# Graph kernel, adjacency build: attribute steps taken in pairs in every second strip, four buffers for the destination one-hots

## The reference, cut to what matters

```python
# x (3125, 128); src, dst (103125,), sorted by dst; edge_attr (103125, 16)
h = jnp.maximum(_layernorm(x), 0.0)
for l in range(5):
    edge_emb = edge_attr @ ew.T + eb
    agg_x = segment_sum(h[src], dst, n) + h
    agg_e = segment_sum(edge_emb, dst, n) + eb
    z = concatenate([agg_x, agg_e], axis=1) @ w1.T + b1
    z = relu((z - mean(z)) * rsqrt(var(z) + 1e-5) * bn_w + bn_b)
    h = z @ w2.T + b2          # relu after layers 0 to 3
return x + h
```

## Time and profile before

| what | value |
|---|---|
| median of 3 runs | 722.11 us |
| the three runs | 726.42, 719.08, 722.11 us |
| the profiled execution, its own time | 723.33 us |
| span of its trace | 721.5 us |
| mean granted clock of TensorE | 0.969 |

### The profile page before, as it was taken

How to read it: one execution, slowest core, us unless ns; L and a number is a source line. 1 busy time by engine, 2 the same in 40 slices (tenths; PEclk the granted TensorE clock), 3 DMA queues, 4 the chain that set the end, 5 groups by cost and what they waited for, 6 DMA issues and landing times.

```text
span 721.5 us, 13619 instructions
## 1 busy us (share of the span) xinstructions
PE 649.8 (90%) x5338; PEld 411.5 (57%) x5338; DVE 382.1 (53%) x807; ACT 260.7 (36%) x627; POOL 89.6 (12%) x62
## 2 busy tenths in 40 slices
PE   0688899898999996989999799997999997999976
PEld 0567678675666663475555665553855556555546
DVE  3699999998999996752120440212421204311124
ACT  0135457675666661470110620113510106201132
POOL 3431226692101110000000000000000000000000
PEclk9899999998999999899999999999999998999998
DMA  8680000000000000000000000000000000100032
GB/s 211 176 261 2 3 2 3 2 3 0 3 1 1 2 1 3 0 8 24 2 1 0 1 29 0 0 0 0 29 0 0 0 0 0 29 2 1 1 89 90
DMA packets 16617, 17.67 MB, mean 24 GB/s; under 512 B 6777, under 2 KB 10786, under 8 KB 16562
## 3 DMA queue, kind: packets, MB, share of 16 engines
q1 hardware_dynamic: 12284, 13.64, 6.4%
q0 software_dynamic: 3440, 1.66, 1.0%
q10 hardware_dynamic: 838, 1.60, 0.8%
HBM read 15.26 MB, written 1.60 MB: 23 GB/s over the span
## 4 chain that ended last, share of the span: by engine, by line
PE 55%; DVE 3%; ACT 1%; issue 0%; POOLq 0%; DVEq 0%
PE bank L961 37%; PE bank L1025 9%; PE bank L996 7%; PE bank L990 2%; DVE bn_stats L1189 1%; ACT h L1079 1%; DVE h L1210 0%; PE bank L1001 0%; ACT aggT L1070 0%; DVE h L1211 0%; ACT bn_small L1092 0%; PE bank L1008 0%; DVE h L1229 0%; DVE bound_row L1169 0%; DVE bn_small L1205 0%
## 5 line engine op out<-in xcount | busy, mean ns | idle before, releaser
L961 PE MATMUL bank<-adj,h_pieces 128*128 (+1 forms) x1400 | 270.8, 353 | 0.0
L961 PEld LDWEIGHTS bank<-adj,h_pieces 128*128 128x128 f16 x1400 | 135.8, 97 | 134.2 <-issue 8.7
L1189 DVE BATCH_NORM_STATS2 bn_stats<-bank 128x6 f32<-128x450 f32 (+1 forms) x70 | 43.8, 629 | 233.9 <-PE bank L996 230.0
L640 ACT ACTIVATE adj<-bank 128x450 bf16<-128x450 f32 x175 | 96.3, 550 | 99.6 <-PE bank L532 99.0
L1070 ACT ACTIVATE aggT<-bank 128x450 f32<-128x450 f32 x28 | 15.3, 546 | 275.9 <-PE bank L996 242.4
L532 PE MATMUL bank<-h 128*128 128x150 bf16 x1050 | 102.3, 234 | 12.8 <-DVE h L301 11.2
L301 DVE TENSOR_TENSOR h<-iota_a,key_a 128x900 bf16<-128x900 bf16 x175 | 110.3, 630 | 0.0
L532 PEld LDWEIGHTS bank<-h 128*128 128x128 bf16 x1050 | 73.0, 99 | 54.2 <-DVE h L301 41.2
L301 DVE TENSOR_TENSOR h<-iota_lo,h 128x768 bf16<-128x768 bf16 x175 | 99.6, 569 | 3.8 <-PE bank L532 1.9
L555 PE MATMUL bank<-h,adj 128*17 128x40 f32 (+11 forms) x1752 | 77.9, 201 | 21.6 <-DMA adj<-attr 19.3
L555 PEld LDWEIGHTS bank<-h,adj 128*17 128x17 f32 x1752 | 68.4, 100 | 31.4 <-DVE h L412 22.1
(11 more groups left out here) (115 smaller groups left out, 307.8 us busy)
## 6 DMA issues: line engine op xcount, KB each, us to landing
adj<-attr SPq DMA_DIRECT2D x5, 1402.5 KB, 15.9
weights<-wpack SPq DMA_DIRECT2D x5, 323.0 KB, 3.2
out<-h SPq DMA_DIRECT2D x6, 256.0 KB
h<-mpack SPq DMA_DIRECT2D x5, 179.0 KB, 2.4
adj<-dst SPq DMA_DIRECT2D x1, 412.5 KB, 12.5
adj<-first SPq DMA_DIRECT2D x1, 201.0 KB, 3.7
adj<-dst_lin,row_index POOLq DMA_INDIRECT x5, 6.8
adj<-pair,start_index POOLq DMA_INDIRECT x5, 11.2
```

Of the source, the lines that this page charges most:

```text
L640: nc.scalar.activation(out_view(u), bank_view(u % CNT_BANKS), ACT.Copy, accum_out=tot[:, u:u + 1]).then_inc(s_ev, 1)
L961: last = nc.tensor.matmul(agg_ps[b][:, 0:CW], hp[:, k, s, :], adj[:, k, ds(c * CW, CW)], start=(k == 0 and s == 0), stop=stop and s == PIE ...
L1189: V.bn_stats(stats[:, h, ds(c * 6, 6)], w1_ps[b][h][:, 0:cols]).then_inc(st_last if last and h == 1 else st_done, 1)
```

## The change

A new constant `DST_SLOTS = 4` gives `dst_oh` four buffers; step `i` on DVE now waits for step `i - 4`. A new function `steps_at(u)` says which steps stand in strip `u`: none in even strips, `u + 3` and `u + 4` in odd ones. DVE and PE both go by it. `step_strip` follows: a chunk that was finished in an even strip now counts from the next odd one. The scratch begins at chunk 1 of `agg0` instead of chunk 3, since four buffers need more room. The number of instructions of each kind is the same.

```diff
+DST_SLOTS = 4
...
+def steps_at(u):
+
+    return [i for i in (u + LEAD - 1, u + LEAD) if i < STEPS] if u % 2 else []
+
+
 def step_strip(i):
 
-    return max(i - LEAD, 0)
+    return max(i - LEAD + (i - LEAD + 1) % 2, 0)
...
-            tail = 3 * CW
+            tail = CW
             sums = agg0[0:REC, tail:tail + CW]
-            dst_oh = agg0[:, tail + CW:tail + CW + SLOTS * RUN * DW].rearrange("p (b x) -> p b x", b=SLOTS)
-            at = tail + CW + SLOTS * RUN * DW
+            dst_oh = agg0[:, tail + CW:tail + CW + DST_SLOTS * RUN * DW].rearrange("p (b x) -> p b x", b=DST_SLOTS)
+            at = tail + CW + DST_SLOTS * RUN * DW
...
-                        if i >= SLOTS:
-                            dve.wait_ge(s_step, i - 1)
+                        if i >= DST_SLOTS:
+                            dve.wait_ge(s_step, i - DST_SLOTS + 1)
...
-                        if u + LEAD < STEPS:
-                            dst_one_hots(u + LEAD)
+                        for i in steps_at(u):
+                            dst_one_hots(i)
...
-                        if u + LEAD < STEPS:
-                            attr_step(u + LEAD)
+                        for i in steps_at(u):
+                            attr_step(i)
```

More of the change, by code:

```diff
@@ L407, in dst_one_hots @@
                     def dst_one_hots(i):
-                        if i >= SLOTS:
-                            dve.wait_ge(s_step, i - 1)
+                        if i >= DST_SLOTS:
+                            dve.wait_ge(s_step, i - DST_SLOTS + 1)
                         k, t = i // 3, (i % 3) * RUN
-                        V.tensor_tensor(dst_oh[:, i % SLOTS, :].rearrange("p (q w) -> p q w", q=RUN),
+                        V.tensor_tensor(dst_oh[:, i % DST_SLOTS, :].rearrange("p (q w) -> p q w", q=RUN),
                                         iota_d.unsqueeze(1).to_broadcast([P, RUN, DW]),
@@ L556, in attr_step @@
                                                         attr_i[:, k, t * REC:(t + 1) * REC],
-                                                        dst_oh[:, i % SLOTS, q * DW + a - c0:q * DW + b - c0],
+                                                        dst_oh[:, i % DST_SLOTS, q * DW + a - c0:q * DW + b - c0],
                                                         start=opens, stop=True, skip_group_check=True)
```

## The result

| | before | changed |
|---|---|---|
| first comparison, median | 722.56 us (4 runs) | 729.62 us (4 runs) |
| first comparison, ratio and 95% interval | | 1.0093 [1.0059, 1.0128] |
| second comparison, median | 723.93 us (23 runs) | 728.32 us (7 runs) |
| second comparison, ratio and 95% interval | | 1.0080 [1.0043, 1.0117] |
| profiled execution, its own time | 723.33 us | 728.73 us |

The ratio is an estimate of its own and not the quotient of the two medians (728.32 / 723.93 is 1.006). By it the change makes the kernel 0.8 to 0.9% slower; the medians lie 7.1 and 4.4 us apart. I had forecast no change, with 728.0 us as the upper end of the range.

What follows compares the result with a forecast made beforehand. DVE, which never rests, was taken to set the build's pace. Terms 0 + 0.1 + 0.5 + 0 = +0.6 us on the profiled 723.33 gave 723.9, in terms of the median 722.7 us, no change; range 717.5 to 728.0 us.

Steps and rivals of the forecast that it cites:

- Part 1: Attribute steps in pairs in the build: DVE needs 3.06 us for two strips before and after; no net gain, 0.
- Part 2: The stack's matmuls on PE, now always behind two attribute steps: DVE may wait, +0.1 us, bounds 0 and 0.5.
- Part 3: Step moved past keys and starts at the end of strip 10: DVE loses +0.5 us, bounds 0 and +0.5.
- Part 4: POOL beside DVE in the build: they lock each other out, equally often in both kernels, so 0.
- rival 1: POOL starves until strip 74, first products on PE start late: +4.4 to +6.3, 727.1 to 729.0 us; chance 0.10.
- Rival 2: PE's clock falls to 1.2 GHz, priced over strips 10 to 17: +6.4 us, 729.1 us or more; chance 0.08.
- rival 3: POOL finishes low pieces while DVE waits anyway, PE's clock does not fall at 160 to 166: 718.2 us; chance 0.10.

## Why the prediction was wrong

**Part 1 held.** Two one-hots stand together, two strips take 3.07 us (from 127.71 to 130.78 us), DVE's wait ahead of the strips is gone and the one for the first pairs grew from 3.19 to 5.58 us, where I forecast about 5.2. Four buffers alone changed nothing.

**Part 2 held.** From the first one-hot to strip 73 the trace lists no wait of DVE for PE. What I missed is that the waits of 0.06 us, which I counted as no cost, had a use.

**Part 3 held in size and missed a place.** The keys' wait grew from 1.44 to 1.79 us and strip 12 began 0.4 us late, where I took 0.5; but since it stays with pairs in even strips, the cause that I gave is not confirmed. Another fixed wait stood at strip 38, where DVE now waits 0.53 us for ACT's deviation, which ACT begins at 106.18 instead of 105.17, behind a copy of the stack that the pairs had moved next to it: 0.6 us that were not in the sum. With pairs in even strips it is gone.

**The step that failed is Part 4's "so I take 0"**, and behind it the sentence in rival 1 that "the gap that let POOL in comes from strips 70 on, which the change leaves as they are". The trace before has two gaps, near 129.8 and 160.7. I priced the second and did not ask what had opened the first, which stood between the row of 114.56 and that of 130. It was the slack of 1.54 us used up by the stack; the pairs put two one-hots between, the gap closed, and POOL was shut out for 43.7 us. Pairs without the extra buffers do it, and holding POOL back in the old order costs the same, 728.5 us. The term that I took as 0 measured 1.4 us in the build of the first profile (6.1 won up to strip 74, 7.5 lost behind it) and 2.4 us in the second (6.1 and 8.5); the other 1.0 and 1.3 us of the build had been lost by strip 40.

**Rival 1 was the right mechanism, at a chance of 0.10.** It had the wait at strip 74 and 727.1 to 729.0 us. PE waited 6.40 us at the first product, which came at 170.02 instead of the 171.4 that I had worked out. PE did restart at its lower clock, as the rival's upper end supposed, until 172.9. The build lost 2.4 and 3.6 us in two profiles, less than the 4.4 of the rival: DVE came to strip 74 at 159.82, 5.1 us ahead of the kernel before and not 2.0, and POOL got in there, 3 us before PE began to count that strip at 162.69.

**The rest of the profiles' difference is the layers' clock, which was no term at all.** In the first profile it brought 3.0 of 5.4 us, in the second 0.7, and since it moves from execution to execution, neither is shown to be an effect of the change. I had read the granted clock as a matter of the build alone. What stays open is how the medians divide: they differ by 7.1 and 4.4 us, the builds of the profiles by 2.4 and 3.6, and the executions without a profile have no record of their layers.

**Rival 2 did not happen**: the granted clock was 1.00 from 60 to 140 us. Neither did rival 3.

## What to carry to other kernels

A short wait on the engine that sets the pace can be what lets another engine at a shared resource in. Before closing it, look which long rows of the other engine end there and who waits for the work queued behind them. Work that must be done by a fixed point should not be left to an engine that gets on only through such gaps: 4.4 us on the busy engine were cheaper here than starving.

When the order of steps changes, list every wait with a fixed place and count how much work stands ahead of it in either order. And where an engine idles once a layer and its clock falls and rises again, two executions of one kernel can differ by 1 to 3 us in a part that no edit touched. So a difference of that size between two profiles is not yet an effect of the edit: look where the granted clock fell and rose in each.

## What the runs showed of the hardware

- One addition on POOL of 128x128 takes 0.4 us while DVE stands still (from 169.84 on in the changed kernel) and 0.5 to 0.8 beside it. Beside DVE instructions with two SBUF inputs that followed each other without a gap it stood for 43.7 us, and for 47.9 where DVE made the low pieces too. The 43.7 us ended when DVE waited 0.41 us for PE ahead of 159.82, 84 instructions later. The lock for one whole instruction that the Trainium skill states ("SBUF — State Buffer", section "Who interferes with whom") fits roughly what DVE pays in a meeting, 0.93 us beside a low piece that takes 1.1 while DVE stands still, and these runs contradict it for POOL's wait.
- The same 100 f32 matmuls behind an idle time of 3.7 us took between 11.5 and 14.2 us, by how much of them stood at the lower clock level (granted clock 1.00 and 0.81 over them).
- The moments at which the granted clock changes are not tied to the kernel: beside strips that started within 0.1 us of each other it fell at 164.30 in one execution and at 164.88 in another, and rose at 171.12 and 168.29. One build was 1.3 us longer by that alone.
